# Rotary attention on one core: TensorE's work of a pair regrouped by tile shape, one key projection split into column halves, copies assigned by position

## The reference, cut to what matters

```python
x = x + attn(_layernorm(x))
q, k, v = split_heads(x @ Wq), split_heads(x @ Wk), split_heads(x @ Wv)
q, k = apply_rope(q), apply_rope(k)
sim = einsum('bid,bjd->bij', q, k) * 64 ** -0.5
attn = softmax(where(causal, sim, -inf), axis=-1)
out = einsum('bij,bjd->bid', attn, v) merged over heads @ Wo + bo
```

## Time and profile before

| what | value |
|---|---|
| device time, three runs | 4271.9, 4279.96, 4286.19 us (median 4279.96) |
| span of the profiled execution, first to last instruction | 4275.1 us (its whole time is not given apart) |
| rotary attention in that span | from about 1250 to 2894 us |
| busy share of the whole span | PE 86%, PEld 51%, DVE 65%, ACT 52%, POOL 45% |
| mean granted clock of TensorE over the span | 0.913 of full speed |

### The profile page before, as it was taken

One profiled execution on the slowest core, in us unless ns is written; L12 is line 12 of the kernel. 1 busy time (PEld: TensorE's weight loads), 2 busy tenths in 40 slices (PEclk: granted clock), 3 DMA queues, 4 the chain that ended last, 5 costly groups with the idle time before them and its releaser, 6 DMA issues. The chain is left out here.

```text
span 4275.1 us, 89510 instructions
## 1 busy us (share of the span) xinstructions
PE 3658.2 (86%) x31167; PEld 2189.1 (51%) x31167; DVE 2761.7 (65%) x6182; ACT 2243.4 (52%) x5440; POOL 1942.7 (45%) x1927
## 2 busy tenths in 40 slices
PE   6999999965959999999999999997666777797768
PEld 1333333324935555555555555556664566575546
DVE  6888888845446666666666666655455665565465
ACT  2666666742415555555555555553225554475367
POOL 2222222117426666656665666656541121466075
PEclk7999999975979999999999999995788998797979
DMA  5333333312642111111111111112452222110000
GB/s 97 57 57 58 59 58 61 50 33 65 209 129 49 40 42 44 45 41 40 44 44 43 40 41 45 44 32 73 153 179 54 67 70 51 35 61 6 1 1 40
DMA packets 418239, 252.25 MB, mean 59 GB/s; under 512 B 251186, under 2 KB 344354, under 8 KB 416642
## 3 DMA queue, kind: packets, MB, share of 16 engines
q1 hardware_dynamic: 409156, 228.56, 23.0%
q0 software_dynamic: 8640, 17.97, 1.3%
HBM read 75.12 MB, written 41.75 MB: 27 GB/s over the span
## 5 line engine op out<-in xcount | busy, mean ns | idle before, releaser
L2495 POOL TENSOR_TENSOR ra_prob<-ra_prob,ra_inverse 128x256 f32<-128x256 f32 (+3 forms) x512 | 639.6, 1253 | 636.2 <-DVE ra_inverse L2689 478.4
L2651 ACT ACTIVATE ra_prob<-ra_ps_s,ra_low 128x128 f32<-128x128 f32 (+3 forms) x1024 | 534.0, 530 | 739.6 <-DVE ra_low L2663 739.5
L2311 DVE TENSOR_REDUCE ca_mx<-ca_ps_s 128x2 f32<-128x1024 f32 x512 | 600.9, 1212 | 111.6 <-PE ca_ps_s L2172 111.2
L2237 ACT ACTIVATE ca_pT<-ca_ps_p 128x512 f32<-128x512 f32 x1024 | 547.8, 601 | 220.5 <-PE ca_ps_p L2182 218.6
L2663 DVE TENSOR_REDUCE ra_low<-ra_ps_s 128x2 f32<-128x256 f32 (+3 forms) x512 | 408.2, 818 | 310.7 <-PE ra_ps_s L2577 309.6
L2172 PE MATMUL ca_ps_s<-ca_kst,ca_qst 128*128 128x512 bf16 x1024 | 395.6, 392 | 37.2 <-DVE ca_mx L2311 20.9
L2519 PE MATMUL ra_ps_t<-ident,ra_prob 128*128 128x128 f32 x2560 | 364.2, 281 | 44.3 <-ACT ra_probT L2629 36.4
L2182 PE MATMUL ca_ps_p<-ca_qst,ca_kst 128*128 128x512 bf16 x1024 | 386.1, 382 | 4.0 <-ACT ca_pT L2237 3.9
L2519 PEld LDWEIGHTS ra_ps_t<-ident,ra_prob 128*128 128x128 f32 x2560 | 273.3, 141 | 213.6 <-ACT ra_probT L2629 83.5
L2577 PE MATMUL ra_ps_s<-ra_kz,ra_qz 64*128 64x128 f32 (+3 forms) x2048 | 381.0, 470 | 0.0
L2591 PE MATMUL ra_ps_o<-ra_probT,ra_v 128*64 128x512 f32 (+3 forms) x2048 | 331.7, 445 | 0.0
(11 more groups left out here) (411 smaller groups left out, 7272.0 us busy)
## 6 DMA issues: line engine op xcount, KB each, us to landing
moe_w_own<-moe_w1T SPq DMA_DIRECT2D x142, 256.0 KB
ra_qz<-ra_rot SPq DMA_DIRECT2D x512, 64.0 KB, 2.0
ra_kz<-ra_rot SPq DMA_DIRECT2D x512, 64.0 KB, 2.0
ca_kst<-ca_bounce SPq DMA_DIRECT2D x256, 64.0 KB
ca_bounce<-ca_thirds SPq DMA_DIRECT2D x192, 64.0 KB, 3.0
ca_qst<-ca_bounce SPq DMA_DIRECT2D x64, 192.0 KB
moe_hs<-moe_rows SPq DMA_DIRECT2D x142, 66.0 KB
moe_raw<-in_L_ffn_W SPq DMA_DIRECT2D x32, 256.0 KB, 2.9
```

What stands on the lines that cost most here:

```text
L2237: nc.scalar.activation(pT[:, (NS * hp + u) % PRING, :], ps_p[n % NP][:], ACT.Exp).then_inc(sg["drained"], 1)
L2311: nc.vector.tensor_reduce(mx[:, hm % 2, 2 * j:2 * j + 2], ps_s[m % 2][:].rearrange("p (b k) -> p b k", b=2), AX.X, ALU.max)\
L2495: nc.gpsimd.tensor_tensor(at, at, inverse[:, n % PROB, 2 * tile:2 * tile + 2].unsqueeze(2).broadcast_to([P, 2, keys]), ALU.mult)\
L2651: nc.scalar.activation(prob[:, score % PROB, t, head, 0:keys], part(score, t)[:, head, :], ACT.Exp, bias=low[:, score % PROB, at:at + 1], ...
```

## The change

TensorE's order in a pair becomes: t=0: projection, mask and scores of tiles 0 and 1, then transposes 0 and 1; t=1: projection, transposes 2 and 3; t=2: projection, transpose 4, the masks of tiles 2 and 3, then the scores of tiles 2 and 3; t=3: projection, then all four value products. The projections by slot become q, v, q, k (first, as two 64-column halves), k, v, output. Fills 0, 2 and 4 of every pair are copied by VectorE, 1 and 3 by ScalarE. The other engines' lists follow: VectorE puts the multiplications and the output addition first in a slot and takes reciprocals for two tiles at a time (two for a pair, not four); ScalarE takes the exponentials of tile 0 ahead of its copy at t=0, the copy of v and the exponentials of tile 1 ahead of its copy at t=1, and tiles 2 and 3 at t=3; GpSimd divides tiles 2 and 3 of the pair before at t=1 (ahead of the query rotation at j=2) and tiles 0 and 1 at t=3. Cut to its core:

Definitions, the GpSimd helper:

```diff
+        COPIED = (3, 2)
+        copied = lambda n, i: (sg["probT_act" if i % 2 else "probT_dve"], COPIED[i % 2] * n + i // 2 + 1)
+        bank_of = lambda n, i: (FILLS * n + i) % 2
...
+                def divide(n, half):
+                    pool.wait_ge(sg["inverse_done"], 2 * n + half + 1)
+                    for tile in (2 * half, 2 * half + 1):
```

GpSimd's list of a slot, then TensorE's waits and projections:

```diff
+                    if front is not None and j == 4:
+                        rotate(front, 1)
...
+                    if t == 1 and 0 <= s - SCORE - 1 < PAIRS:
+                        divide(s - SCORE - 1, 1)
+                    if front is not None and j == 2:
+                        rotate(front, 0)
+                    if t == 3 and score is not None:
+                        divide(score, 0)
...
-                    wait(pe, sg["probT_act" if f % 2 else "probT_dve"], f // 2)
+                    if f >= 2:
+                        pe.wait_ge(*copied((f - 2) // FILLS, (f - 2) % FILLS))
...
+                    elif unit == 2:
+                        pe.wait_ge(sg["v_ready"], 2 * k + 1)
                     else:
+                        pe.wait_ge(sg["multiplied"], 8 * k + {1: 2, 3: 4, 4: 6, 5: 8}[unit])
+                    if unit in (1, 5):
...
+                    elif unit == 3:
+                        for side in range(2):
+                            at = slice(side * DH, (side + 1) * DH)
+                            last = nc.tensor.matmul(ps_r[at, :], w[:, 1, 0, k % NQ, at], xT[:, b % 2, :], start=True, stop=True)
+                        last.then_inc(sg["qk_in"], 1)
```

TensorE's list of a slot:

```diff
-                    if value is not None:
-                        for i in fills(t):
-                            turn(i, value)
-                    if score is not None and t == 2:
-                        scores(t, score)
                     if front is not None and j < 6:
                         project(j, front)
...
+                    if score is not None and t == 0:
+                        masks(0, score)
+                        scores(0, score)
+                    if value is not None:
+                        for i in fills(t):
+                            turn(i, value)
+                    if score is not None and t == 2:
+                        for tile in (2, 3):
+                            masks(tile, score)
+                        for tile in (2, 3):
+                            scores(tile, score)
+                    if value is not None and t == 3:
+                        for at in range(TC):
                             values(at, value)
```

ScalarE's list of a slot (the copy of v stands where a line of dots follows t == 1):

```diff
+                    if score is not None and t == 0:
+                        exponentials(0, score)
+                    if value is not None and t == 0:
+                        fill(1, value)
+                    if front is not None and t == 1:
...
+                    if score is not None and t == 1:
+                        exponentials(1, score)
+                    if value is not None and t == 1:
+                        fill(3, value)
...
+                    if score is not None and t == 3:
+                        exponentials(2, score)
+                        exponentials(3, score)
```

VectorE's list of a slot (the output addition stands where a line of dots follows j == 6):

```diff
+                    if front is not None and j in (0, 2, 4):
+                        multiply(j, front)
+                    if out is not None and j == 6:
...
+                    if score is not None and t == 0:
+                        minima(0, score)
+                    if value is not None and t < 3:
+                        fill(2 * t, value)
+                    if t == 1 and 0 <= s - SCORE - 1 < PAIRS:
+                        invert(s - SCORE - 1, 1)
                     if score is not None and t == 2:
+                        minima(2, score)
+                        invert(score, 0)
+                    if front is not None and j == 3:
+                        multiply(3, front)
+                    if score is not None and t == 3:
+                        minima(3, score)
```

More of the change, by code:

```diff
@@ L2496, in body @@
                             .then_inc(sg["divided"], 1)
+                def body(j, t, s, front, score, value, out, batch):
+                    if front is not None and j == 4:
+                        rotate(front, 1)
                     if batch is not None and j == 4:
@@ L2560, in turn_rows, with masks @@
                     last.then_inc(sg["x_turned"], 1)
-                def scores(t, n):
+                def masks(t, n):
                     if t == 0:
@@ L2621, in _, with exponentials, fill @@
                             .then_inc(w_ready, 1)
-                def body(j, t, s, front, score, value, out, batch):
[L2624 to L2629, removed]
+                def exponentials(tile, n):
+                    keys = (tile + 1) * P
+                    act.wait_ge(sg["low_done"], TC * n + max(tile, 1) + 1)
+                    wait(act, sg["p_turned"], FILLS * (n - PROB + 1))
+                    wait(act, sg["inverse_done"], 2 * (n - PROB + 1))
+                    for head in range(2):
+                        at = 2 * tile + head
+                        nc.scalar.activation(prob[:, n % PROB, tile, head, 0:keys], part(n, tile)[:, head, :], ACT.Exp,
+                                             bias=low[:, n % PROB, at:at + 1], scale=-1.0, accum_out=total[:, n % PROB, at:at + 1]).then_inc(sg["exp_done"], 1)
+                def fill(i, n):
+                    act.wait_ge(sg["p_turned"], FILLS * n + i + 1)
+                    wait(act, sg["pv_done"], TC * (n - 1) + used(i))
+                    nc.scalar.copy(probT[:, i, :], ps_t[bank_of(n, i)][:]).then_inc(sg["probT_act"], 1)
+                def body(j, t, s, front, score, value, out, batch):
                     done = s - VALUE - 1
@@ new lines, in multiply @@
+                def multiply(unit, front):
+                    o, nth, x = {0: (0, 0, 0), 2: (0, 1, 1), 3: (1, 2, 0), 4: (1, 3, 1)}[unit]
+                    dve.wait_ge(sg["qk_in"], 4 * front + nth + 1)
+                    wait(dve, sg["rotated"], 4 * (front - 1) + 2 * (o + 1))
+                    first, second = (prod[:, o, 0, :], prod[:, o, 2, :]) if x == 0 else (prod[:, o, 3, :], prod[:, o, 1, :])
+                    nc.vector.tensor_tensor(first, ps_r[:], cos[:], ALU.mult).then_inc(sg["multiplied"], 1)
+                    nc.vector.tensor_tensor(second, ps_r[:], sin[:], ALU.mult).then_inc(sg["multiplied"], 1)
```

107 lines of the change are left out of this document (35 added, 72 removed).

## The result

The changed kernel takes **4254.7 us** (median of 4 runs, 4252.3 to 4257.9) against 4277.3 before: ratio 0.9944, 95% interval 0.9928 to 0.996, a gain of 17 to 31 us. The direction was forecast, the size was not: 57 us were forecast, 23 came, and 4254.7 lies inside the range of 4170 to 4278.

What follows compares the result with a forecast made beforehand. TensorE's in-order list was taken as the bound. Four quads: 4 x 23.79 + 2.4 = 97.6 against 101.25 us, 15.5 times, -57; span about 4218, plus 4.9: 4223 us. Own range 4205 to 4260; nearly all outcomes 4170 to 4278.

Steps and rivals of the forecast that it cites:

- The quad: Two pairs, output projection to output projection, no change of sequence: 23.79 us, 1.15 less than 24.94.
- 1.32 of shapes: TensorE changes matmul shape five times a pair instead of nine, saving drain and late starts: 1.32 us a quad.
- 0.90 of new stall: TensorE waiting ahead of transposes 2 and 3 for VectorE's and ScalarE's copies: 0.45 us in every pair.
- The hand-over chain: From the projection at t=0 through VectorE and ScalarE until TensorE gets `ps_r` back for t=2: 5.25 us.
- The shapes: Expected shape-change costs a quad: 0.19 us for an undivided key projection, 0.49 for tile 3's scores back at t=3.
- rival B: Key projection's column halves run one behind the other: +0.86 us a quad, +53 in all, 4276 us; 6%.
- Rival C: Key DMAs land late, so TensorE's masks at t=0 and everything behind them wait: slower, 4341 us; 8%.
- Rival A: The stall at t=1 is covered and TensorE alone binds: 0.45 us less in each pair, 4168 us; 8%.
- Change of sequence, once in four quads: Extra time from variance, normalization and transposed rows where the sequence changes: 2.4 us, where before had 1.49.
- Sum 2.4: Total us for a change of sequence: 0.3 variance, 1.5 wait, 0.49 work, 0.1 drain.
- 1.5 of wait: At j=7 TensorE arrives at 9.6 us, the second normalization ends at 11.1: 1.5 us wait ahead of transposed rows.
- the 0.3 for the variance: VectorE's variance at the end of j=3, ahead of the multiplication at j=4: 0.3 us of its 1.13 counted.

Runs made afterwards that it cites:

- e5: Kernel before with one part alone: VectorE copies fills 0, 2, 4 of every pair, ScalarE 1 and 3; 4271.0 us, ratio 0.9973.
- e6: Changed kernel with copies swapped: ScalarE takes fills 0, 2, 4 (fill 0 ahead of tile 0's exponentials), VectorE 1 and 3; 4203.4 us.
- e8: e6 plus reciprocal root ahead of key rotation, all four normalizations at j=5, division of tiles 2 and 3 waiting for them; 4148.4 us.
- e3: Changed kernel with the key projection at j=3 as one 128-column matmul instead of two column halves; 4250.9 us, ratio 0.993.
- e1: Changed kernel with GpSimd's division of tiles 2 and 3 waiting for the first two normalizations at a change of sequence; 4216.7 us.
- e9: Changed kernel with three unread 128x512 fp32 matmuls put into TensorE's wait ahead of the transposed rows; 4230.2 us, ratio 0.9888.
- e4: On top of e3, the scores of tile 3 and their masks moved back to t=3; 4332.1 us, ratio 1.0119 against the kernel before.

## Why the prediction was right in direction and wrong in size

*Right.* The quad: 23.79 forecast, 23.72 measured. What it is made of was not all seen: 1.32 of shapes less 0.90 of new stall makes 0.42, not the 1.15 forecast. The rest is, but for 0.08, an old stall of 0.65 in each quad of before (e5), which the sum from rows left out without naming it. By the runs a quad lost this stall (0.65), lost 1.50 by the new order (24.29 in e5, 22.79 in e6) and got 0.93 of new stall (22.79 in e6, 23.72): 1.22 in all. The hand-over chain: 5.25 against 5.24, and e6 and e8 show that it was the bound of t=1. The shapes: 0.19 forecast for the halves, 0.21 measured; 0.49 for the scores, 0.56 measured. The halves run side by side: their matmuls start 7 ns apart, both halves take 0.91 us, and e3 shows them worth a gain, not a pass. So rival B falls. The Trainium skill, TensorE: Matmul & The Clock Gate, Part 3 (The mechanism), states the rule from which it came, that a weight load overlaps with running matmuls only where the row group differs. This trace does not agree: the weight loads of the second passes start at 1824.23, while the first passes of both halves run (from 1824.18; the second passes start at 1824.66). Rival C did not come: between 1300 and 2860 us no wait of TensorE ends with a key DMA. Rival A did not come by itself; e6 made it, with 22.79 where A's sum has 23.79 - 0.90 = 22.89.

*Wrong.* The step that failed is "Change of sequence, once in four quads", its term "Sum 2.4", measured 4.1: (4.1 - 2.4) x 15.5 = 26 us of the 34 that are missing between 57 and 23. In its own terms: "1.5 of wait" ahead of the rows measured 2.70, the 0.3 for the variance came to nothing, and the clock, not in the sum, took 0.75 in the mean. Two things were left out. First, the first two normalizations. I set the division "from 5.5 to 8.9" for all pairs; where the sequence changes, the root stands ahead of it, both then become free at the same moment, and VectorE's loses. I had priced the second pair at the 1.30 of rows 6 and not asked why the 64 normalizations of before, 0.32 to 1.06 us each, differ, nor why four columns of variance took 1.13. The division also goes through in one group of 3.3 us now, not a tile at a time. e1 shows 2.4 us of extra from this, clock included. Second, the clock: I named a clock under 1.00 as a sign that I was wrong, and gave it no price; a wait that grew from 0.57 to 2.70 us brought it to the lower level in every second change, 0.75 us in the mean (e9).

Rotary attention alone became 33 us shorter: 57 less these 26, and 0.07 in a plain quad (4 us in all) in its favour makes 35, and 34 with the fifteen changes of sequence that ran instead of 15.5. Between 33 and the 23 of the whole lie 10 us of the rest of the program, 14 us longer in this profile than in that of before, with no line of it changed. What moves the rest was not tried.

## What to carry to other kernels

Sum the rare case as carefully as the plain one: the change of sequence, once in four quads, took back 2.6 of the 4.9 us that the four had gained. When work on two engines is regrouped into longer runs, ask which instruction of the other engine now starts beside such a run, and look in the trace for one instruction with two durations: the longer one names its partner. An in-order engine that waits pays twice if its clock falls behind the wait, so put the late work behind work that is ready, or make it early.

## What the runs showed of the hardware that was not expected

A normalization of 128x128 on VectorE takes 0.3 us alone and 1.49 and 1.93 us beside divisions of 1.47 and 1.90 us on GpSimd; the division lost nothing. A wait of 2.70 us on TensorE brought the lower clock behind every second occurrence and not behind the others, though both came 7.09 us after the same instruction; with 1.07 us (e1) or with matmuls in the wait (e9) it came behind none. In the other kernels it came behind eight of fifteen waits of 1.83 us (e5), seven of fifteen of 2.59 (e6), ten of fifteen of 2.70 (e3) and all fifteen of 3.67 (e4). The same untouched instructions of the rest took between 2626 and 2645 us from kernel to kernel.
